# One merge of three edits: split first gathers, the last block written out with one linear half moved behind its squares, and a new order around the expert weights

## The chip, the cores and the metric

The kernel runs on one core of one Trainium2 chip. The metric is the device time of one execution in microseconds (us), the median of three runs. Engines are named as the profile names them: PE (TensorE, matrix products), DVE (VectorE), ACT (ScalarE), POOL (GpSimd) and SP (SyncE, which here only issues transfers).

## The reference

Input x has 64 samples of 64 x 512 numbers, which is 4096 rows of 512. Cut to what matters:

```
# layer 0
w   = weights[subjects]                         # 8 matrices of 64 x 64, one chosen for each sample
y   = einsum('bct,bcd->bdt', x, w)              # the "mix"
gu  = y @ ternary(w_gate_up).T                  # 512 -> 4096, gate and up
h   = silu(gate) * up                           # 2048 wide
x1  = x + rms_norm(h) @ ternary(w_proj).T       # 2048 -> 512
# layer 1
h   = x1 @ W.T + scal * (x1 @ A_b.T) @ B_b.T    # a linear layer, with one of 8 adapters per sample
logits = (h @ router_w.T + router_b)            # for each of 512 outputs, 8 experts
c   = per token: sum over the outputs of the renormalised top-2 weights, for each of 8 experts
out = x1 + sum_e c[t, e] * (h[t] @ expert_w[e].T + expert_b[e])
```

## The kernel before

Every float32 product is made of two or three products of rounded parts: a value is split into a high part and a remainder (`_hi`, `_lo`), so each large product is a chain of PE matmuls of 128 x 512, with a weight load each. ACT writes the high part (a copy), DVE subtracts it to get the low part. Nothing is scheduled by a tool. Each of the five engines has its own instruction list, written by hand in the order of the code, and semaphores counted in program order set who waits for whom. The numbers that the waits use for the two PSUM slots of stage 1 come from the lists `FIRST`, `SECOND`, `REST` and `TAIL` through `use(i, name)`: the n-th use of the slots may be written when use n-2 has been drained.

**Stage 1 (to about 900 us).** The 4096 rows go in 8 blocks of 512. For one block i, PE does `mix(i)` (L1420), then 16 hidden chunks `gu(i, j)` (L1445, 16 matmuls each), each followed by `proj(i, j-1)` (L1458, 8 matmuls), and in between the layer-1 linear part of block i-1: `turn` (transposes, L1477), `adapt` (L1487) and the two halves of `linear` (L1498 to L1504, 30 matmuls each), at j = 5 and j = 7. ACT and DVE store each half with `store_h` and `split_h`: ACT copies the high part, DVE subtracts, and ACT issues four transfers of 256 KB to `h_scratch`. After the last chunk come `proj(i, 15)`, `squares(i)` (L1467, the sum for the norm) and DVE's `finish(i)` (L1099, L1103), which takes an inverse root from POOL and writes x1. Blocks 0 and 1 are written out; in them the ternary weights are made (`quant`, L1430 on PE, with ACT and DVE). Blocks 2 to 7 are a loop on PE, DVE and ACT.

At the very start SP issues eight small gathers of the 64 x 64 matrices of block 0 (`gather_mix`, L415 to L417: a register load and a transfer for each sample), then two weight loads, the x rows of block 1, and eight gathers for block 1. ACT loads its first two function tables where it first needs them.

**Passage to stage 2 (898 to 942 us).** When the last `gu` has been drained SP loads 8 MB of router weights (`rraw`, one MB for each expert) over the old stage-1 weights. ACT and DVE split them (L830, L1198) while PE finishes block 7: transposes, the first group of router products, adapter, both linear halves.

**Stage 2 (to about 1628 us).** 32 tiles of 128 rows: PE makes router logits in PSUM planes (L1576 to L1580), ACT evacuates and seeds with the bias, DVE finds the top two of eight (`half`, L1267 to L1291), ACT and DVE pack them as bit codes (`stand`, `join`), and SP spills them.

**Passage to stage 3 and stage 3.** SP loads 8 MB of expert weights (`eraw`, L548). ACT and DVE split them (L913, L1332). Then 32 tiles again: PE makes eight expert products per tile (`experts`, L1618 to L1622, 12 matmuls per expert, 96 per tile), DVE adds each, scaled, to an accumulator (`expert`, L1371), ACT writes the expert bias back into the freed PSUM bank (`seed_expert`, L942), which is what PE waits for before it writes that bank again. In between DVE makes the scale factors of the tile after next (`decode`, L1236 to L1249, and eight times `total`, L1304). For tile 0 the bias isn't seeded: DVE adds it with eight instructions of its own (`bias`, L1353).

Of the kernel before, what the change touches and what calls it, by code (L numbers as in the profile page):

```python
# [29 lines left out]
P = 128  # L30
D = 512
# [73 lines left out]
TAIL = ["ss", "t0", "t1", "xa", "h0", "h1"]  # L105
# [24 lines left out]
def use(i, name):  # L130


    if isinstance(i, int):
        if i < 2 and f"{name}@{i}" in FIRST:
            n = FIRST.index(f"{name}@{i}")
        elif i == 0:
            n = FIRST.index(name)
        elif i == 1:
            n = len(FIRST) + SECOND.index(name)
        elif i == NBLK:  # L140
            n = len(FIRST) + len(SECOND) + (NBLK - 2) * len(REST) + TAIL.index(name)
        else:
            n = len(FIRST) + len(SECOND) + (i - 2) * len(REST) + REST.index(name)
# [18 lines left out]
def build(nc, x, idx7, idx6, cond_w, w_ffn, WcT, AT, Bt, scal, rwT, rb, ewT, eb, out):  # L162
# [7 lines left out]
    with root:  # L170
# [81 lines left out]

        bias_sb = sb("bias_sb", [P, 2, E, HO], F32, p2)
# [7 lines left out]
        c_ring = sb("c_ring", [P, 4, E], F32, p2)  # L261
        p3 = ExitStack()
        eb_sb = sb("eb_sb", [P, E, D], F32, p3)
# [4 lines left out]
        L = sb("L", [P, 2, E, HO], F32, p2)  # L268
# [35 lines left out]
        mixw_in = sem("mixw_in")  # L304
        xres_in = sem("xres_in")
# [21 lines left out]
        q_step = sem("q_step")  # L327
        mean_ready = sem("mean_ready")
# [63 lines left out]
        EWT = ewT.rearrange("(c p) (e o) -> e p c o", p=P, o=D)  # L392
# [19 lines left out]
        def _(sp):  # L412
            def gather_mix(i, w, done):
                for q in range(SPB):
# [25 lines left out]
            gather_mix(0, mixw, mixw_in)  # L440
# [116 lines left out]
            sp.wait_ge(decoded, 2)  # L557
            load_halves(2)
            spill(NT - 1, 1, 2 * NT - 1, 2 * NT, 2 * NT)

            def ahead(n, u, wait):

                if isinstance(n, int) and n == 0:
                    sp.wait_ge(bias_step, 1)
                else:
                    sp.wait_ge(exp_step, wait)
# [29 lines left out]
        def _(pool):  # L596
            nc.gpsimd.iota(adapter_i[:, :], pattern=[[0, 1]], base=0, channel_multiplier=1).then_inc(consts, 1)
# [20 lines left out]
        def _(act):  # L618
# [67 lines left out]
            def square(i, j, h):  # L686

                if not (first_block(i) and j == 0):
# [120 lines left out]
            with act.Fori(2, NBLK) as i:  # L809
                mix(i)  # L810
                for j in range(HC):
# [26 lines left out]
            split_router(1)  # L838
            store_x1(NBLK - 1)
# [10 lines left out]
            split_router(5)  # L850
            copy_h(NBLK - 1, 0)
# [79 lines left out]
            def store(n, u):  # L931
                act.wait_ge(exp_step, n * E + E)
# [12 lines left out]
            with act.Fori(0, NT // 2 - 1) as m:  # L945
                for u in range(2):
                    weigh(m * 2 + (u + 2), u, m + 1)
                    for e in range(E):
                        seed_expert(m * 2 + u, e)
                    store(m * 2 + u, u)  # L950
                    load_h(m * 2 + (u + 2), u)
            for e in range(E):
# [715 lines left out]
```

## Time and profile before

| | |
|---|---|
| median of three runs | 2350.64 us (2349.07 to 2351.0) |
| the profiled execution's own time | 2351.97 us |
| its span, first to last instruction | 2350.2 us |
| PE busy | 2301.7 us, 98% |
| DVE busy | 1669.3 us, 71% |
| ACT busy | 1148.8 us, 49% |
| mean granted TensorE clock | 0.995 |

The times of a row are microseconds from the start of the span. In a row of the timeline, the figure in brackets is how long the engine had stood idle before that row, and what released it. PE is idle for about 48 us in all, and nearly all of it lies in four places: the first 50 us, the end of block 7, the start of the experts, and the last 4 us.

### The profile page before, as it was taken

The page shows a single profiled execution, that of the slowest core. Times are in us where ns is not written, and L with a number is a line of the kernel's source. Part 1 is how long each engine was busy: PE and PEld are TensorE (multiplying, and loading weights), DVE is VectorE, ACT ScalarE, POOL GpSimd, SP SyncE. Part 2 cuts the span into 40 slices and gives each one's busy share as a digit, 9 for nine tenths or more (in the row PEclk, how much of TensorE's full clock was granted, in tenths as well). Part 3 has the DMA queues.
Part 4 walks back from the last instruction along what each step waited for, and adds up shares of the span by engine and source line. Part 5 has one row for each costly group of instructions (what it writes and reads, how often), then busy time and mean ns, then how long its engine had stood idle before and what let it go on. Part 6 is the DMA issues. An engine that isn't in the chain of part 4 may idle for free.

```text
span 2350.2 us, 30421 instructions
## 1 busy us (share of the span) xinstructions
PE 2301.7 (98%) x10280; PEld 1897.4 (81%) x10288; DVE 1669.3 (71%) x2497; ACT 1148.8 (49%) x1685; POOL 8.9 (0%) x16
## 2 busy tenths in 40 slices
PE   6999999999999999999999999998899999999999
PEld 5777888888888887888888888887688888888887
DVE  7985434334343435888888888999988888888883
ACT  6764333323332324788888888887322222222221
POOL 0000000000000000000000000000000000000000
PEclk9999999999999999999999999999999999999999
DMA  5314202111111115211111111215322222222220
GB/s 197 105 44 137 74 19 74 43 54 51 54 54 37 71 36 201 75 65 62 62 54 66 58 58 63 67 62 182 142 91 87 94 78 78 94 80 76 94 80 22
DMA packets 106589, 184.61 MB, mean 79 GB/s; under 512 B 12466, under 2 KB 45746, under 8 KB 105266
## 3 DMA queue, kind: packets, MB, share of 16 engines
q1 hardware_dynamic: 54946, 124.84, 15.2%
q10 hardware_dynamic: 51600, 59.25, 7.6%
q8 instruction: 20, 0.33, 0.1%
q14 instruction: 23, 0.19, 0.0%
HBM read 122.72 MB, written 61.34 MB: 78 GB/s over the span
## 4 chain that ended last, share of the span: by engine, by line
PE 90%; issue 5%; DVE 3%; ACT 1%; DMA 1%; ACTq 0%; SPq 0%; POOL 0%; POOLq 0%; DVEq 0%
PE slot L1445 17%; PE plane L1576 10%; PE plane L1578 10%; PE plane L1580 10%; PE ex L1618 10%; PE ex L1620 10%; PE ex L1622 10%; PE pj L1458 8%; PE slot L1498 3%; PE slot L1420 1%; PE slot L1487 1%; PE slot L1477 1%; PE slot L1430 0%; DMA eraw<-in_ewT 0%; DMA eb_sb<-in_eb 0%
## 5 line engine op out<-in xcount | busy, mean ns | idle before, releaser
L1618 PE MATMUL ex<-ew_hi,hb 128*128 128x512 f32 x1024 | 400.8, 391 | 16.6 <-DVE ew_lo L1332 11.3
L1445 PE MATMUL slot<-y_hi,wgu 128*128 128x512 f32 x1024 | 403.1, 394 | 2.3 <-DVE q_scale L1002 1.2
L1576 PE MATMUL plane<-rw_hi,hb 128*128 128x512 f32 x1024 | 399.5, 390 | 1.6 <-ACT plane L834 0.9
L1620 PE MATMUL ex<-ew_hi,hb 128*128 128x512 f32 x1024 | 400.4, 391 | 0.0
L1622 PE MATMUL ex<-ew_lo,hb 128*128 128x512 f32 x1024 | 400.3, 391 | 0.0
L1578 PE MATMUL plane<-rw_hi,hb 128*128 128x512 f32 x1024 | 399.2, 390 | 0.0
L1445 PE MATMUL slot<-y_lo,wgu 128*128 128x512 f32 x1024 | 399.1, 390 | 0.0
L1580 PE MATMUL plane<-rw_lo,hb 128*128 128x512 f32 x1024 | 399.1, 390 | 0.0
L942 ACT ACTIVATE ex<-eb_sb 128x512 f32<-128x512 f32 x248 | 149.3, 602 | 460.0 <-DVE acc L1371 395.8
L1304 DVE SCALAR_TENSOR_TENSOR lead_in<-code_in,wts 128x1024 bf16<-128x1024 bf16 x256 | 311.5, 1217 | 1.8 <-DVE code_in L1249 0.4
L1618 PEld LDWEIGHTS ex<-ew_hi,hb 128*128 128x128 f32 x1024 | 193.4, 189 | 58.5 <-issue 7.9
L1044 DVE TENSOR_TENSOR hid<-gate,slot 128x512 f32<-128x512 f32 x112 | 76.9, 687 | 222.8 <-ACT gate L673 222.1
L1445 PEld LDWEIGHTS slot<-y_hi,wgu 128*128 128x128 f32 x1024 | 192.3, 188 | 46.0 <-DVE q_scale L1002 4.3
L673 ACT ACTIVATE gate<-slot 128x512 f32<-128x512 f32 x128 | 76.5, 598 | 310.6 <-PE slot L1445 263.4
L1576 PEld LDWEIGHTS plane<-rw_hi,hb 128*128 128x128 f32 x1024 | 192.7, 188 | 42.4 <-ACT plane L834 1.3
L1622 PEld LDWEIGHTS ex<-ew_lo,hb 128*128 128x128 f32 x1024 | 193.5, 189 | 40.5
L1620 PEld LDWEIGHTS ex<-ew_hi,hb 128*128 128x128 f32 x1024 | 193.4, 189 | 40.2
L1580 PEld LDWEIGHTS plane<-rw_lo,hb 128*128 128x128 f32 x1024 | 192.7, 188 | 40.2
L1578 PEld LDWEIGHTS plane<-rw_hi,hb 128*128 128x128 f32 x1024 | 192.8, 188 | 40.0
L1445 PEld LDWEIGHTS slot<-y_lo,wgu 128*128 128x128 f32 x1024 | 192.3, 188 | 39.7
L862 ACT ACTIVATE L<-plane 128x512 f32<-128x512 f32 x256 | 150.5, 588 | 109.6 <-PE plane L1580 104.2
L1371 DVE SCALAR_TENSOR_TENSOR acc<-ex,c_ring,acc 128x512 f32<-128x512 f32 x193 | 144.5, 748 | 69.8 <-PE ex L1622 66.9
(128 smaller groups left out, 3148.3 us busy)
## 6 DMA issues: line engine op xcount, KB each, us to landing
hb<-h_scratch SPq DMA_DIRECT2D x34, 512.0 KB, 3.3
h_scratch<-ht ACTq DMA_DIRECT2D x64, 256.0 KB, 3.0
code_scratch<-half_code SPq DMA_DIRECT2D x64, 256.0 KB, 2.0
half_in<-code_scratch SPq DMA_DIRECT2D x32, 512.0 KB, 3.3
hb<-h_scratch ACTq DMA_DIRECT2D x30, 512.0 KB, 3.6
q_raw<-in_w_ffn SPq DMA_DIRECT2D x21, 512.0 KB, 3.4
x_scratch<-x_res ACTq DMA_DIRECT2D x8, 1024.0 KB, 4.4
rraw<-in_rwT SPq DMA_DIRECT2D x8, 1024.0 KB, 11.0
```

The lines of the kernel that those rows point to most:

```text
L862: nc.scalar.activation(L[:, s, 2 * b:2 * b + 2, :], plane[b][:, :, :], ACT.Copy).then_inc(evac, 1)
L942: nc.scalar.activation(ex[e][:, :], eb_sb[:, e, :], ACT.Copy).then_inc(ex_seeded, 1)
L1304: nc.vector.scalar_tensor_tensor(lead_in[:, k % 2, :].bitcast(BF16).rearrange("p (a n) -> p a n", a=2), code_in[:, k % 2, :, :], float(2 * ...
L1371: nc.vector.scalar_tensor_tensor((res if e == E - 1 else acc)[:, u, :], ex[e][:, :], c_ring[:, k, e:e + 1], base[:, u, :], ALU.mult, ALU.a ...
L1445: last = mm(slot[s % 2][:, g, :], wgu[:, c, r * P:(r + 1) * P], y[:, c, :], start=(c == 0 and v == 0), stop=(c == DC - 1 and v == 1))
L1458: last = mm(pj[k][:, :], h[:, k * P:(k + 1) * P], wpj[:, w, :], start=(j == 0 and v == 0), stop=(j == HC - 1 and v == 1))
L1576: mm(plane[b][:, :, :], hb[:, u, c, 0, :], rw_hi[:, w, c, o], start=False, stop=False, skip_group_check=True)
L1578: mm(plane[b][:, :, :], hb[:, u, c, 1, :], rw_hi[:, w, c, o], start=False, stop=False, skip_group_check=True)
L1580: last = mm(plane[b][:, :, :], hb[:, u, c, 0, :], rw_lo[:, w, c, o], start=False, stop=True, skip_group_check=True)
L1618: mm(ex[e][:, :], hb[:, u, c, 0, :], ew_hi[:, e, c, :], start=(first and c == 0), stop=False, skip_group_check=True)
L1620: mm(ex[e][:, :], hb[:, u, c, 1, :], ew_hi[:, e, c, :], start=False, stop=False, skip_group_check=True)
L1622: last = mm(ex[e][:, :], hb[:, u, c, 0, :], ew_lo[:, e, c, :], start=False, stop=(c == DC - 1), skip_group_check=True)
```

## The change

The layout of the lists is changed so that block 7 is numbered apart. Its loop trip is written out on PE, DVE and ACT (`block(NBLK - 1)`), without the second linear half of block 6, which each of the three engines now does after the squares of block 7. The first gathers are shared between SP and POOL, ACT's Silu table is loaded first, and SP's first transfers are reordered. The expert weights are laid out so that one expert's 1 MB is contiguous for each partition; they are loaded in one run. In the first expert tile PE does all products with the high part of the weights first, and then those with the low part. DVE adds the expert bias of tile 0 after its expert sums, and the packing of the last two router halves, the decoding and the totals of tile 2 follow. Buffers are moved so that the bias table of the experts lies over that of the router and can be loaded earlier.

```diff
-TAIL = ["ss", "t0", "t1", "xa", "h0", "h1"]
+LAST = [name for name in REST if name != "h1"]
+TAIL = ["ss", "last h1", "t0", "t1", "xa", "h0", "h1"]
...
-            gather_mix(0, mixw, mixw_in)
+            gather_mix(0, mixw, mixw_in, range(SPB // 2))
...
+            sp.dma_start(x_res[:, :, :], one(XB, 1)).then_inc(xmix1_in, 16)
+            gather_mix(1, mixw1, mixw1_in, range(3))
             load_raw(3)
             load_raw(4)
-            sp.dma_start(x_res[:, :, :], one(XB, 1)).then_inc(xmix1_in, 16)
-            gather_mix(1, mixw1, mixw1_in)
+            gather_mix(1, mixw1, mixw1_in, range(3, SPB))
...
-                    sp.dma_start(eraw[:, e, :, :], EWT[e]).then_inc(eraw_in[e], 16)
-                if b == 0:
-                    spill(NT - 2, 0, 2 * NT - 3, 2 * NT - 2, 2 * NT - 2)
+                    sp.dma_start(eraw[:, e, :, :].rearrange("p c o -> p (c o)"), ewT[e]).then_inc(eraw_in[e], 16)
             load_h(1, 1)
-            sp.wait_ge(joined, 2 * NT)
-            sp.dma_start(xin[:, 0, :], X1T[0]).then_inc(x1_in[0], 16)
+            sp.wait_ge(seeded, NT * PT)
             sp.dma_start(eb_sb[:, :, :], eb).then_inc(eb_in, 16)
-            sp.dma_start(xin[:, 1, :], X1T[1]).then_inc(x1_in[1], 16)
+            spill(NT - 2, 0, 2 * NT - 3, 2 * NT - 2, 2 * NT - 2)
             load_lead(2, 0)
             sp.wait_ge(decoded, 2)
             load_halves(2)
+            sp.wait_ge(lead_ready, 2 * NT)
+            sp.dma_start(xin[:, 0, :], X1T[0]).then_inc(x1_in[0], 16)
+            sp.dma_start(xin[:, 1, :], X1T[1]).then_inc(x1_in[1], 16)
             spill(NT - 1, 1, 2 * NT - 1, 2 * NT, 2 * NT)
...
         def _(pool):
+            pool.wait_ge(dconst, 1)
+            pool.wait_ge(subject_in, 16)
+            for q in range(SPB // 2, SPB):
+                v = pool.value_load(subject_i[0:1, q:q + 1], min_val=0, max_val=E - 1)
+                r = (q % 2) * C
+                pool.dma_start(mixw[r:r + C, q // 2, r:r + C], cond_w[bass.ds(v * C, C), :]).then_inc(mixw0_in, 16)
...
+            act.wait_ge(dconst, 3)
+            nc.scalar.activation(sq[:, 0:1], ones_col[:, :], ACT.Silu).then_inc(table_in, 1)
             quant_in(0)
...
-            with act.Fori(2, NBLK) as i:
+            def block(i):
...
-                    if j == 7:
+                    if j == 7 and not isinstance(i, int):
                         store_h(i - 1, 1)
+
+            with act.Fori(2, NBLK - 1) as i:
+                block(i)
                 act.wait_ge(h_stored, i * 128)
+            block(NBLK - 1)
...
             split_router(0)
             split_router(1)
+            store_h(NBLK - 2, 1)
             store_x1(NBLK - 1)
...
             split_router(5)
+            act.wait_ge(h_stored, 128 * (NBLK - 1))
             copy_h(NBLK - 1, 0)
...
-            split_expert(2)
+            for e in range(2, E):
+                split_expert(e)
             stand(NT - 1, 0)
-            split_expert(3)
-            split_expert(4)
             stand(NT - 1, 1)
-            for e in range(5, E):
-                split_expert(e)
...
             finish(NBLK - 1)
             split_router(0)
+            split_h(NBLK - 2, 1)
             split_router(1)
...
+            for e in range(E):
+                expert(0, e, 0, 0)
+            for s in range(2):
+                join(NT - 1, s)
             dve.wait_ge(eb_in, 16)
+            dve.wait_ge(exp_step, E)
             for e in range(E):
-                bias(0, e, 0, 1)
-            for n in range(4):
+                bias(e)
+            decode(2, 2)
+            for e in range(E):
+                total(2, e, 2)
+            for n in range(1, 4):
                 tile(n, n, n // 2)
...
+            linear(NBLK - 2, 1)
             turn(NBLK - 1, 0)
...
+            def first_experts():
+
+                pe.wait_ge(hb_in[0], NT // 2 * 16 + 16)
+                for e in range(E):
+                    if e >= 4:
+                        pe.wait_ge(evac, NT * PT - 3 + e - 4)
+                    pe.wait_ge(ehi, e + 1)
+                    for c in range(DC):
+                        for v in range(2):
+                            mm(ex[e][:, :], hb[:, 0, c, v, :], ew_hi[:, e, c, :], start=(c == 0 and v == 0), stop=False)
+                for e in range(E):
+                    pe.wait_ge(elo, e + 1)
+                    for c in range(DC):
+                        last = mm(ex[e][:, :], hb[:, 0, c, 0, :], ew_lo[:, e, c, :], start=False, stop=(c == DC - 1))
+                    last.then_inc(ex_filled, 1)
```

The order of ACT at the end of block 7, before: the router weights' high parts, the store of x1 (`x_scratch`), the first seed (`plane`), the two turns.

```order
L830 ACTIVATE rw_hi<-rraw 128x2048 x2
L749 DMA x_scratch<-x_res 128x4x512
L834 ACTIVATE plane<-bias_sb 128x512
L717 ACTIVATE x1t_hi<-slot 128x1024 x2
L830 ACTIVATE rw_hi<-rraw 128x2048 x2
```

The same place now:

```order
L849 ACTIVATE rw_hi<-rraw 128x2048 x2
L744 ACTIVATE ht<-slot 128x2x512
L753 DMA h_scratch<-ht 128x4x128 x4
L762 DMA x_scratch<-x_res 128x4x512
L853 ACTIVATE plane<-bias_sb 128x512
L730 ACTIVATE x1t_hi<-slot 128x1024 x2
L849 ACTIVATE rw_hi<-rraw 128x2048 x2
```

The copy of the moved half and its four transfers stand ahead of the store of x1, the seed and the turns.

The order of DVE from the low parts of the expert weights (`ew_lo`) to the second tile, before (the first part of `half`, nine rows, left out; L1353 is the bias, L1371 an expert sum, L1304 a total):

```order
L1230 TENSOR_TENSOR half_code<-sgn 128x1024
L1286 TENSOR_TENSOR L<-L,m 128x1024
L1287 TENSOR_TENSOR L<-L,m 128x1024
L1291 TENSOR_TENSOR lead<-m 128x256
L1332 TENSOR_TENSOR ew_lo<-eraw,ew_hi 128x2048 x2
L1230 TENSOR_TENSOR half_code<-sgn 128x1024
L1332 TENSOR_TENSOR ew_lo<-eraw,ew_hi 128x2048 x3
L1353 SCALAR_TENSOR_TENSOR acc<-eb_sb,c_ring,xin 128x512
L1353 SCALAR_TENSOR_TENSOR acc<-eb_sb,c_ring,acc 128x512 x7
L1371 SCALAR_TENSOR_TENSOR acc<-ex,c_ring,acc 128x512
L1236 TENSOR_TENSOR half_in<-half_in 128x2x512
```

The same place now:

```order
L1325 TENSOR_TENSOR lead<-m 128x256
L1366 TENSOR_TENSOR ew_lo<-eraw,ew_hi 128x2048 x5
L1395 SCALAR_TENSOR_TENSOR acc<-ex,c_ring,xin 128x512
L1395 SCALAR_TENSOR_TENSOR acc<-ex,c_ring,acc 128x512 x7
L1264 TENSOR_TENSOR half_code<-sgn 128x1024 x2
L1380 SCALAR_TENSOR_TENSOR acc<-eb_sb,c_ring,acc 128x512 x7
L1380 SCALAR_TENSOR_TENSOR res<-eb_sb,c_ring,acc 128x512
L1270 TENSOR_TENSOR half_in<-half_in 128x2x512
```

The expert sums of tile 0 stand ahead of the two joins (`half_code`) and of the bias, and the totals that stood between them follow in one run.

## Rows read from the trace of the kernel before

**Rows 1.** Waits of PE: total us, times, longest us.
```profile
PE ex L1618 <- DVE ew_lo L1332: 11.3, 2, 7.3
...
PE ex L1618 <- ACT ex L942: 5.3, 2, 3.2
```
**Rows 2.** Stretches: us; busy PE, PEld, DVE, ACT, POOL; clock; DMA share; GB/s.
```profile
50.00:100.00 50.00, 49.73 (x217) 39.04 (x220) 45.47 (x68) 36.53 (x48) 0.00 (x0) 1.00 0.33 111
...
912.00:914.00 2.00, 2.00 (x6) 1.56 (x5) 2.00 (x3) 2.00 (x2) 0.00 (x0) 0.50 1.03 430
```
**Rows 3.** Timeline of the start: SP, PE, DVE, ACT.
```profile
3.02 9.36 SPq L417 DMA_DIRECT2D mixw<-in_cond_w  x8
...
10.22 1.04 PE L1430 MATMUL slot<-q_mag,group_mean 128*128 128x512 bf16 x2 [3.95 <-DMA mixw<-in_cond_w]
13.98 5.70 PE L1420 MATMUL slot<-mixw,x_mix 128*128 128x128 f32 x32 [2.72 <-issue]
...
15.46 0.69 DVE L1030 TENSOR_TENSOR q_res<-q_res,q_sign 128x1024 bf16<-128x1024 bf16 x1
28.36 0.69 DVE L1044 TENSOR_TENSOR hid<-gate,slot 128x512 f32<-128x512 f32 x1 [0.97 <-ACT gate L673]
...
26.44 1.28 ACT L673 ACT_TABLE_LOAD   x1
```
**Rows 4.** Tile mixw in the first 45 us: its gathers' time to landing.
```profile
DMA to landing us min/median/max: 1.8/2.6/6.4
```
**Rows 5.** Timeline, end of block 7: PE, then ACT.
```profile
906.62 3.68 PE L1477 MATMUL slot<-ident,x_res 128*128 128x128 f32 x16 [4.10 <-DVE x_res L1103]
...
916.03 0.40 PE L1487 MATMUL slot<-x1t_hi,a_hi 128*128 128x512 f32 x1
...
942.03 0.50 PE L1576 MATMUL plane<-rw_hi,hb 128*128 128x512 f32 x1 [0.88 <-ACT plane L834]
...
926.02 1.03 ACT L731 ACTIVATE ht<-slot 128x1024 fp32r<-128x1024 f32 x1 [0.47 <-PE slot L1504]
930.71 3.72 ACT L830 ACTIVATE rw_hi<-rraw 128x2048 fp32r<-128x2048 f32 x2 [3.66 <-issue]
```
**Rows 6.** Chain of waits: twelve matmuls of a linear half.
```profile
278.79 2.80 PE slot L1498 x12
```
**Rows 7.** Tile x_scratch: time to landing of its transfers.
```profile
DMA to landing us min/median/max: 2.5/2.9/16.5
```
**Rows 8.** Timeline of DVE, from the expert weights to tile 1.
```profile
1628.17 1.22 DVE L1304 SCALAR_TENSOR_TENSOR lead_in<-code_in,wts 128x1024 bf16<-128x1024 bf16 x1
...
1629.32 4.49 DVE L1332 TENSOR_TENSOR ew_lo<-eraw,ew_hi 128x2048 fp32r<-128x2048 f32 x2
...
1637.37 1.22 DVE L1267 TENSOR_TENSOR top<-L 128x1024 f32<-128x1024 f32 x1
...
1646.73 4.48 DVE L1332 TENSOR_TENSOR ew_lo<-eraw,ew_hi 128x2048 fp32r<-128x2048 f32 x2
1651.13 0.68 DVE L1230 TENSOR_TENSOR half_code<-sgn 128x1024 uint16<-128x1024 uint16 x1
1652.84 6.69 DVE L1332 TENSOR_TENSOR ew_lo<-eraw,ew_hi 128x2048 fp32r<-128x2048 f32 x3 [1.03 <-ACT ew_hi L913]
...
1660.89 5.48 DVE L1353 SCALAR_TENSOR_TENSOR acc<-eb_sb,c_ring,acc 128x512 f32<-128x512 f32 x7
...
1671.64 0.75 DVE L1371 SCALAR_TENSOR_TENSOR acc<-ex,c_ring,acc 128x512 f32<-128x512 f32 x1
...
1684.27 0.75 DVE L1371 SCALAR_TENSOR_TENSOR acc<-ex,c_ring,xin 128x512 f32<-128x512 f32 x1
...
1689.49 0.75 DVE L1371 SCALAR_TENSOR_TENSOR acc<-ex,c_ring,acc 128x512 f32<-128x512 f32 x1
```
**Rows 9.** Timeline of PE in the first expert tiles.
```profile
1673.07 0.52 PE L1618 MATMUL ex<-ew_hi,hb 128*128 128x512 f32 x1 [2.14 <-ACT ex L942]
...
1696.58 0.39 PE L1618 MATMUL ex<-ew_hi,hb 128*128 128x512 f32 x1
```

More of the change, by code:

```diff
@@ L139, in use @@
             n = len(FIRST) + SECOND.index(name)
-        elif i == NBLK:
-            n = len(FIRST) + len(SECOND) + (NBLK - 2) * len(REST) + TAIL.index(name)
+        elif i == NBLK or (i == NBLK - 1 and name == "h1"):
+            n = len(FIRST) + len(SECOND) + (NBLK - 3) * len(REST) + len(LAST) + TAIL.index(name if i == NBLK else "last h1")
+        elif i == NBLK - 1:
+            n = len(FIRST) + len(SECOND) + (NBLK - 3) * len(REST) + LAST.index(name)
         else:
@@ L412, in _, with gather_mix @@
         def _(sp):
-            def gather_mix(i, w, done):
-                for q in range(SPB):
+            def gather_mix(i, w, done, samples=range(SPB)):
+                for q in samples:
                     v = sp.value_load(subject_i[0:1, bass.ds(i * SPB + q, 1)], min_val=0, max_val=E - 1)
@@ L686, in square @@
             def square(i, j, h):
-                if not (first_block(i) and j == 0):
+                if first_block(i) and j == 0:
+                    act.wait_ge(table_in, 1)
+                else:
                     act.wait_ge(ss_ready, i * HC + j)
@@ L1180, in _, with block @@
                     split_h(0, 1)
-            with dve.Fori(2, NBLK) as i:
+            def block(i):
                 mix(i)
@@ L1191, in _ @@
                         split_h(i - 1, 0)
-                    if j == 7:
+                    if j == 7 and not isinstance(i, int):
                         split_h(i - 1, 1)
+            with dve.Fori(2, NBLK - 1) as i:
+                block(i)
+            block(NBLK - 1)
             def split_router(e):
@@ L1336, in _, with bias @@
                 split_expert(e)
-            half(NT - 1, 1, 1, NT // 2 - 1)
-            split_expert(3)
-            split_expert(4)
-            join(NT - 1, 1)
-            for e in range(5, E):
-                split_expert(e)
-            def bias(n, e, k, trip):
-                u = k % 2
-                if e == 0:
-                    dve.wait_ge(x1_in[u], trip * 16)
-                    dve.wait_ge(summed, n * E + E)
-                else:
-                    dve.wait_ge(bias_step, n * E + e)
-                nc.vector.scalar_tensor_tensor(acc[:, u, :], eb_sb[:, e, :], c_ring[:, k, e:e + 1],
-                                               (xin if e == 0 else acc)[:, u, :], ALU.mult, ALU.add).then_inc(bias_step, 1)
+            half(NT - 1, 1, 1, NT // 2 - 1, joins=False)
+            for e in range(3, E):
+                split_expert(e)
+            def bias(e):
+                if e:
+                    dve.wait_ge(bias_step, e)
+                nc.vector.scalar_tensor_tensor((res if e == E - 1 else acc)[:, 0, :], eb_sb[:, e, :], c_ring[:, 0, e:e + 1],
+                                               acc[:, 0, :], ALU.mult, ALU.add).then_inc(bias_step, 1)
             def expert(n, e, k, trip):
                 u = k % 2
-                base = acc
+                first = isinstance(n, int) and n == 0
                 if e != 0:
                     dve.wait_ge(exp_step, n * E + e)
-                elif isinstance(n, int) and n == 0:
-                    dve.wait_ge(bias_step, E)
                 else:
@@ L1370, in expert @@
                     dve.wait_ge(out_done[u], trip * 16)
-                nc.vector.scalar_tensor_tensor((res if e == E - 1 else acc)[:, u, :], ex[e][:, :], c_ring[:, k, e:e + 1],
-                                               base[:, u, :], ALU.mult, ALU.add).then_inc(exp_step, 1)
+                nc.vector.scalar_tensor_tensor((res if e == E - 1 and not first else acc)[:, u, :], ex[e][:, :],
+                                               c_ring[:, k, e:e + 1], (xin if e == 0 else acc)[:, u, :],
+                                               ALU.mult, ALU.add).then_inc(exp_step, 1)
             def tile(n, k, pair):
@@ L1546, in _, with block @@
                     linear(0, 1)
-            with pe.Fori(2, NBLK) as i:
+            def block(i):
                 mix(i)
@@ L1560, in _ @@
                         linear(i - 1, 0)
-                    if j == 7:
+                    if j == 7 and not isinstance(i, int):
                         linear(i - 1, 1)
+            with pe.Fori(2, NBLK - 1) as i:
+                block(i)
+            block(NBLK - 1)
             proj(NBLK - 1, HC - 1)
```

50 lines of the change are left out of this document (26 added, 24 removed).

## The prediction

> **What bounds the kernel now.** I read four views, in this order. The page's busy times name PE as the engine that is nearly always at work, so a change can only win what PE stands idle, or what it loses at a low clock. The waits of PE say what it stands idle for: in [rows 1] the reader is to see two waits for the low parts of the expert weights, 11.3 us together, and two for a PSUM bank that ACT has to seed again, 5.3 us. The view by stretches says where there is nothing to win: PE is busy for 49.73 of the 50 us from 50 to 100 [rows 2], and all over the loops. The timelines of the start, of the end of block 7 and of the first expert tiles then say what ends each wait last. I call a time "old" when it is read on the clock of the trace before.
>
> **Start: gain 2.5 us.** SP issues the eight gathers of block 0 in 9.36 us, 1.17 each, and PE starts the mix at 13.98, after 2.72 us of idleness [rows 3]. Now SP and POOL issue four each. SP's last is issued at 3.02 + 3 x 1.17 = 6.5. POOL issues no transfer anywhere in the trace, so its pace is bounded. At SP's pace and the median landing of 2.6 us [rows 4] all are in at 9.1; but PE itself is busy with the second mean until 11.26 [rows 3], so the mix can start at 11.3 at best, a gain of 2.7. At worst its transfers come only after DVE's run of bf16 instructions, which ends at 15.46 + 0.69 = 16.15 [rows 3]: 16.15 + 2.6 = 18.8, a loss of 4.8. I take a landing near the longest one, 6.0 of the 6.4 us [rows 4], since the weight loads, the x rows and all eight gathers now fall into the same ten microseconds: 6.5 + 6.0 = 12.5, a gain of 1.5. It is nearer to the good end because the only rows of such a gather are SP's. Everything behind follows the mix: ACT and DVE split its output, then go on without a wait for a load.
>
> The tables: ACT loads one at 26.44, 1.28 us, ahead of the first gate, and DVE is idle for 0.97 us before the product with it [rows 3]. Now the table with Silu is loaded first, where the other one was loaded before, and the load at 26.44 is gone. DVE has its own work up to the start of that idleness, so 1.0 us is won and not 1.28. The new one-column Silu delays ACT's first copy by some tenths, which the later wait for the second weight load covers. From there DVE and PE work in step until 50 us, and after it PE is 49.73 of 50 us busy [rows 2], so both gains are passed on: 1.5 + 1.0 = 2.5. If the cover of the first tenths is gone, it costs these tenths.
>
> [...]
>
> **End of block 7: gain 3.1 us.** A linear half is 30 matmuls: 12 take 2.80 us [rows 6], so it is 7.0 us. It goes out of block 7, so all up to the last squares comes 7.0 us earlier, and goes in after the squares, at old 902.5, just where PE waits 4.10 us for x1 [rows 5]. It ends at old 909.5. The first transposes follow (x1 is ready at 906.6), but the second ones need the slot of the moved half drained, and ACT now has to do this half's copy, wait for DVE, and issue four transfers ahead of the seed and the turns. Such a copy started at 926.02 and ACT's next compute instruction at 930.71, so this costs ACT 4.69 us [rows 5]: 909.5 to 914.2, then x1's transfer, about 0.4, the seed, 0.6, and PE's first router group starts at old 915.3. PE has stood idle for some 4 of the 5 us up to there, as much as before 906.62, where the granted clock went to the lower level: at 912 to 914 it is 0.50, and only 6 matmuls start in 2 us [rows 2], where 2.80/12 us each would give 8.6. So I let the group of 12 take 4.3 us. The adapter starts at 919.6; before, it started at 916.03 [rows 5], where the same low clock had slowed the group. Delay 3.6 us. It is carried on: ACT's copy of the next half at 926.02 + 3.7, its loads' high parts 4.69 later, the same chain up to the seed that PE waits for at 942.03 [rows 5], which comes 3.7 to 3.9 us later. Net gain 7.0 - 3.9 = 3.1. If the clock stays high, ACT's chain begins at its two turns and the delay is 2.6: gain 4.4, the upper bound. The lower bound: ACT's next copy now waits for the moved half's transfers to land (they share the buffer). They are issued at old 911.8 to 914.1 into 8 MB of router weights under way; a transfer of x1 issued there needed 16.5 us where 2.9 is the median [rows 7]. 914.1 + 16.5 = 930.6 against 929.7 when it is wanted: a cost of up to 1 us, or 3 us if 1 MB more makes it longer. Lower bound 0.
>
> The Trainium skill, "DMA: Bandwidth & Descriptors", section "Queues, rings and completion order", says that a DMA engine takes turns between the queues packet by packet. The 16.5 us agree with it: x1's packets are smaller than those of the router weights. The packets of the moved half are smaller still (512 bytes of 128 numbers); by this rule it lands last of all, which is rival 2.
>
> **The experts: gain 6.8 us.** Before, PE takes an expert only when its low part is there, and DVE does `half` (1637.37 to 1646.73, 9.36 us) between the third and the fourth low part [rows 8]. Now PE does the 64 high products first, for which ACT's copies suffice, and the low ones as DVE delivers. What then ends last is DVE, and it is busy without a gap, so I add it up from old 1629.32 [rows 8]: three low parts 6.7; `half` without its join 9.36 - 0.6 = 8.8; five low parts 11.1 (up to here 1655.9); eight expert sums at the pace of dependent ones, 5.48/7 = 0.78, 6.3; two joins 1.3; eight of the bias 6.3; decoding 3.4 (the 5.22 below less a sum and a total); eight totals at 1.25, 10.0; this gives 1683.2 for the first expert sum of tile 1, which stood at 1684.27. The second one comes 5.22 later as before (1684.27 to 1689.49), at 1688.4. The seed lies between DVE and PE: DVE's sum at 1671.64, PE at 1673.07, 1.4 us [rows 8, 9]. So PE can start the second expert of tile 2 at 1689.8. Before, it started it at 1696.58 [rows 9], being late itself: it had lost 11.3 + 5.3 us [rows 1] and more at the low clock. The gain is 6.8. PE isn't what ends last: low products done at about 1657, plus 96 matmuls at 0.23, is 1679; it then waits some 5 us for the first seed of tile 2 (1683.2 + 1.4 = 1684.6). Its clock will fall after that, and 12 matmuls at 0.43 us, double 0.21, take 5.1 and end at 1689.7, just when the second seed comes. From there DVE takes 5.22 us once and about 1.8 for each further expert of a tile, which is less than PE's 12 x 0.23 = 2.8, and no wait is left. The weights: 8 MB contiguous, the last 2 MB no later than before; DVE needs the last one at 1653.7. The x1 rows are now asked for at old 1644.7 and needed at 1655.9, behind about 4 MB; if they are late it costs up to 2 us. Bounds 4 and 7.5 us.
>
> **Sum.** 2.5 + 3.1 + 6.8 = 12.4 us. The profiled execution took 2351.97 us, 1.3 more than the median of 2350.64; it would take 2339.6. The median of three becomes 2338.2.
>
> **Rivals.** 1: POOL's descriptors wait for DVE. The mix starts at 18.8, the start costs 4.8 - 1.0 = 3.8 instead of winning 2.5; total gain 3.1 + 6.8 - 3.8 = 6.1, 2344.5 us. For it: DVE's bf16 instructions up to 16.15 [rows 3]; against: each gap between two of them is a chance to get in. 12%. 2: the moved half holds up ACT, by its landing or its place, and block 7 gives nothing: gain 9.3, 2341.3 us. For it the 16.5 us; against, 929.7 is almost late enough. 13%. 3: the run of bias and totals ahead of tile 1 holds PE longer than I sum, because x1's rows or the decoding's inputs land late behind 4 MB, and the low clock then stretches over the second expert: the experts give 3, total 8.6, 2342.0 us. 10%. 4, the other side: block 7 as straight code has to be fetched by three engines, and they starve for instructions. It would have to cost more than 12.4 us to undo the gains, and 17.1 to be measured as slower, in a block of about 100 us (some 426 large matmuls at 0.23). Against it: the stretch from 50 to 100 us is straight code too, and PE is busy for 49.73 [rows 2]. 4%, at some 2360 us. 5: the change does little, since what it wins is lost to waits not seen: 3%, 2349 us. My forecast, all three gains within their middle: 58%.
>
> **How the numbers follow.** About 0.2%, 4.7 us, is what a measurement of this kernel can tell from no change. Forecast and rivals 1 to 3 are all faster by more than that, but for their tails: 88%. Within 0.2%: rival 5 and the tail of rival 1 in company of 2, 7%. Slower: rival 4 and what I don't see, 5%. The range: rivals 1 and 3 inside, best case 2.7 + 1.0 + 4.4 + 7.5 = 15.6 us, 2335.0. From 2334.3 to 2346.0 about one in ten is left out above and less than that below.
>
> **What would show it.** Start: the mix on PE at 11.3 to 13 and one table load on ACT before the gates; at 18 or later rival 1 is right. Block 7: no wait for x1 before the transposes, a wait of about 2.5 us before the first router group, the wait before the second half's groups about 1 us. Experts: 64 high products with waits under 1 us, low ones at DVE's pace of 2.2 us, then one wait of 5 us before tile 2, and DVE without a gap. I am wrong if PE waits in tile 2 for more than the first two experts, or if block 7 isn't shorter by 7 us up to its last squares.

## The result and the profile after

The changed kernel takes 2346.94 us, median of 22 runs (2345.03 to 2350.4); the kernel before takes 2350.61 us beside it (22 runs, 2349.07 to 2352.16). The ratio is 0.9986, 95% interval 0.9979 to 0.9992: 3.3 us less (1.9 to 4.9; the two medians are 3.7 apart), which is within the 0.2% that I had called "no change". The forecast was 2338.2 us with a range up to 2346.0, so three quarters of the expected gain are missing. The profiled execution after took 2350.2 us (span 2348.5), near the slow end of its spread; before it was 2351.97 (span 2350.2), so between the two traces only 1.7 us are gained.

Two places divide the trace into three: A, where PE starts the adapter of block 0 (201.71 before), and B, where it starts the router's second half (s=1, 942.03 in [rows 5]). After, timeline of PE:

```profile
11.90 6.09 PE L1455 MATMUL slot<-mixw,x_mix 128*128 128x128 f32 x32 [0.51 <-DMA mixw<-in_cond_w]
...
200.04 0.47 PE L1522 MATMUL slot<-x1t_hi,a_hi 128*128 128x512 f32 x1 [1.80 <-DVE x1t_lo L1138]
...
902.45 1.03 PE L1512 MATMUL slot<-ident,x_res 128*128 128x128 f32 x8
905.08 1.06 PE L1512 MATMUL slot<-ident,x_res 128*128 128x128 f32 x8 [1.59 <-DVE ht L1157]
915.52 0.76 PE L1615 MATMUL plane<-rw_hi,hb 128*128 128x512 f32 x1 [9.38 <-ACT plane L853]
...
947.32 0.50 PE L1615 MATMUL plane<-rw_hi,hb 128*128 128x512 f32 x1 [1.19 <-ACT plane L853]
```

Up to A it is 1.67 us shorter, from B to the end 6.99 us shorter (1401.18 against 1408.17), and from A to B 6.96 us longer, where I had forecast 3.1 us less. The sum is the 1.7 us. The waits of PE say the same: the two for low parts of [rows 1], 11.3 us, are 1.9 now, the ones for `ex` are about as long as before, five short ones for ACT's high parts of these weights are new (3.4 us, the longest 1.8), and so is a long one for the seed of the first router group.

```profile
PE plane L1615 <- ACT plane L853: 10.6, 2, 9.4
PE ex L1653 <- ACT ex L962: 5.8, 3, 4.8
...
PE ex L1672 <- DVE ew_lo L1366: 1.9, 2, 1.0
```

What holds the seed up is in ACT's timeline (ACTq is the issuing of transfers on ACT):

```profile
902.65 1.02 ACT L744 ACTIVATE ht<-slot 128x1024 fp32r<-128x1024 f32 x1 [2.28 <-PE slot L1539]
904.96 8.67 ACTq L753 DMA_DIRECT2D h_scratch<-ht  x4
913.67 1.06 ACTq L762 DMA_DIRECT2D x_scratch<-x_res  x1
914.78 0.60 ACT L853 ACTIVATE plane<-bias_sb 128x512 f32<-128x512 f32 x1 [11.11 <-issue]
...
931.33 1.03 ACT L744 ACTIVATE ht<-slot 128x1024 fp32r<-128x1024 f32 x1 [0.82 <-PE slot L1539]
933.65 2.31 ACTq L753 DMA_DIRECT2D h_scratch<-ht  x4
```

The four transfers of the moved half take 8.67 us to issue; the same four of the next half take 2.31. By itself each shows that it is the fourth: the first three take 0.38, 0.53 and 0.53 us, the last, in the group below, 7.14.

```profile
L753 ACTq DMA_DIRECT2D h_scratch<-ht x12: 378/532/7141, 905.0 to 945.2; - x12
```

Meanwhile the loads of the router weights fill the DMA engines. The queues between 905 and 910 us, SP's is q1 and ACT's q10 (packets, MB, share), and two stretches as in [rows 2]:

```profile
q1 hardware_dynamic: 286, 2.08, 99.5%
q10 hardware_dynamic: 77, 0.04, 2.6%
```
```profile
908.00:912.00 4.00, 0.00 (x0) 0.00 (x0) 0.00 (x0) 0.00 (x0) 0.00 (x0) 0.50 1.02 421
916.00:920.00 4.00, 4.00 (x11) 3.03 (x10) 3.29 (x3) 4.00 (x4) 0.00 (x0) 0.50 1.10 368
```

ACT's queue moves 0.04 MB in five microseconds, though it has up to 1 MB to move. PE, DVE and ACT all stand still from 908 to 912, and after it PE works at the lower level of its clock (0.50) to about 921: the twelve matmuls of the group start 0.43 us apart and take 5.26 us, to the adapter's first at 920.78.

### The profile page after: what moved, and what is told of

Its sections match the earlier page's. It is cut to its first block, busy times and chain, and to the rows that moved or that the text cites. A ratio compares the mean times of both kernels' runs of the same rounds, so it can differ in the third digit from the quotient of the medians.

```text
span 2348.5 us, 30271 instructions
## 1 busy us (share of the span) xinstructions
PE 2302.6 (98%) x10280; PEld 1895.4 (81%) x10288; DVE 1670.0 (71%) x2497; ACT 1148.0 (49%) x1685; POOL 11.2 (0%) x20
## 4 chain that ended last, share of the span: by engine, by line
PE 94%; DVE 3%; DMA 1%; ACT 1%; issue 1%; ACTq 1%; SPq 0%; DVEq 0%
PE slot L1480 20%; PE plane L1615 10%; PE plane L1617 10%; PE plane L1619 10%; PE pj L1493 9%; PE ex L1653 9%; PE ex L1655 9%; PE ex L1654 9%; PE slot L1533 4%; PE slot L1455 1%; PE slot L1522 1%; DMA eraw<-in_ewT 1%; ACTq L753 1%; PE slot L1512 0%; DVE lead_in L1338 0%
## 5 line engine op out<-in xcount | busy, mean ns | idle before, releaser
L1653 PE MATMUL ex<-ew_hi,hb 128*128 128x512 f32 x992 | 386.9, 390 | 5.8 <-ACT ex L962 5.8
L1654 PE MATMUL ex<-ew_hi,hb 128*128 128x512 f32 x992 | 386.4, 390 | 0.0
L1655 PE MATMUL ex<-ew_lo,hb 128*128 128x512 f32 x992 | 386.4, 390 | 0.0
L1653 PEld LDWEIGHTS ex<-ew_hi,hb 128*128 128x128 f32 x992 | 186.6, 188 | 45.8 <-ACT ex L962 6.4
L1654 PEld LDWEIGHTS ex<-ew_hi,hb 128*128 128x128 f32 x992 | 186.6, 188 | 38.7
L1655 PEld LDWEIGHTS ex<-ew_lo,hb 128*128 128x128 f32 x992 | 186.5, 188 | 38.8
```

The lines of the kernel that those rows point to most:

```text
L1653: mm(ex[e][:, :], hb[:, u, c, 0, :], ew_hi[:, e, c, :], start=False, stop=False, skip_group_check=True)
L1654: mm(ex[e][:, :], hb[:, u, c, 1, :], ew_hi[:, e, c, :], start=False, stop=False, skip_group_check=True)
L1655: last = mm(ex[e][:, :], hb[:, u, c, 0, :], ew_lo[:, e, c, :], start=False, stop=(c == DC - 1), skip_group_check=True)
```

## The experiments

Each part alone and taken out, then the moved half's transfers in other places. Medians in us; A, B and "A to B" are read from the profiled execution of each. A ratio is to the kernel before, measured beside it: its medians were 2351.23 us for e1 to e4, 2350.99 for e5, e6, e9 and e10, and 2351.78 for e7, e8, e11 and e12.

| kernel | median | ratio to before, 95% | A | B | A to B |
|---|---|---|---|---|---|
| before | 2350.61 | | 201.71 | 942.03 | 740.32 |
| changed | 2346.94 | 0.9986 (0.9979 to 0.9992) | 200.04 | 947.32 | 747.28 |
| e1, block 7 undone | 2341.40 | 0.9960 (0.9946 to 0.9974) | 200.19 | 938.35 | 738.16 |
| e2, block 7 alone | 2356.49 | 1.0023 (1.0014 to 1.0032) | 202.85 | 947.75 | 744.90 |
| e3, sends later on ACT | 2339.07 | 0.9951 (0.9938 to 0.9965) | 198.17 | 935.68 | 737.51 |
| e4, sends on SP | 2339.03 | 0.9953 (0.9939 to 0.9966) | 198.20 | 935.36 | 737.16 |
| e5, three there | 2338.38 | 0.9947 (0.9932 to 0.9962) | 198.53 | 934.61 | 736.08 |
| e6, loads held | 2346.16 | 0.9978 (0.9968 to 0.9987) | 200.40 | 944.32 | 743.92 |
| e7, start alone | 2347.72 | 0.9983 (0.9974 to 0.9992) | 199.92 | 938.10 | 738.18 |
| e8, experts alone | 2343.76 | 0.9966 (0.9952 to 0.9979) | 201.78 | 942.08 | 740.30 |
| e9, eight halves | 2346.88 | 0.9984 (0.9975 to 0.9993) | 197.92 | 942.78 | 744.86 |
| e10, group between | 2338.89 | 0.9953 (0.9939 to 0.9966) | 198.50 | 936.00 | 737.50 |
| e11, sends ahead | 2335.24 | 0.9931 (0.9917 to 0.9944) | 199.77 | 933.51 | 733.74 |
| e12, between, on ACT | 2338.37 | 0.9945 (0.9931 to 0.9958) | 197.98 | 934.67 | 736.69 |

### The parts apart: e1, e2, e7, e8

e1 is the changed kernel with block 7 as before, e2 the kernel before with this part alone (the same edit the other way round), on all engines:

```
-                    if j == 7 and not isinstance(i, int):
+                    if j == 7:
                         linear(i - 1, 1)
...
-            linear(NBLK - 2, 1)
             turn(NBLK - 1, 0)
```

This is PE's share; `store_h` on ACT and `split_h` on DVE go the same way.

> The changed kernel with its second part undone: the half linear(6, 1) is back in block 7. Theory A (the fourth transfer of the moved half is held up at its issue on ACT for 7.1 us, since 8 MB of router weights are under way; PE stands idle for 9.4 us; the move costs about 5.3 us): start and experts keep their gains, 2350.6 - 1.7 - 7.1 = 2341.8 us, some 5 us less than the changed kernel; PE waits 4.1 us for x1 before the first transposes as before. Theory B (the long issue is an accident of the one profiled execution, and the rest of the gain went to stretches at the low clock): the move gives its 3.1 us in the median, so without it 2350 us. Theory C (the end of block 7 is worth nothing either way): 2347.

> The kernel before with the move of linear(6, 1) alone, nothing of the start and of the experts. Theory A: the fourth issue takes about 7 us again, PE waits some 9 us for the first seed, and the time is 2350.6 + 5.3 = 2355.9 us. Theory B: 2350.6 - 3.1 = 2347.5 us. Theory C: 2350.6.

Measured: 2341.40 and 2356.49 us, 0.4 less and 0.6 more than theory A gives. Without the move the kernel is faster by 5.5 us than with it; the move alone makes the kernel before slower by 5.3 us (3.3 to 7.5). In the trace of e2 the four issues take 8.68 us and PE waits again:

```profile
906.10 8.68 ACTq L743 DMA_DIRECT2D h_scratch<-ht  x4
```
```profile
916.49 0.77 PE L1594 MATMUL plane<-rw_hi,hb 128*128 128x512 f32 x1 [9.21 <-ACT plane L841]
```

So the long issue is no accident of one execution: theories B and C fall. e7 is the kernel before with `gather_mix(0, ..., range(SPB // 2))`, POOL's four gathers and the early Silu alone; e8 has only the edits at the experts.

> The kernel before with the part at the start alone (four gathers of block 0 on POOL, the Silu table first, the order of SP's first loads). Forecast of the prediction: 2.5 us less, 2348.3. In the traces of the kernels with this part PE reaches the first product of the second block's adapter 1.3 to 1.7 us sooner than before (201.7 us) where a stretch after the mix ran at the low clock, and 3.2 to 3.8 us sooner where it didn't: 2347 to 2349.5. Rival: what the start wins is given back later, 2351.

> The kernel before with the part at the experts alone. Forecast of the prediction: 6.8 us less, 2344.1; the trace of the changed kernel gives 7.1, 2343.8. Rival (the low clock or late rows of x1 eat it): 2347.5 or more.

Measured: 4.0 us less (1.9 to 6.1) for the start, 8.0 us less (4.9 to 11.3) for the experts. Neither is given back later. But the trace of e7 has only 1.8 us of its gain at A; 2.1 more come at the end of block 7, where nothing was changed. There PE waits the same 4.10 us for x1, but is back at the full clock when the first router group starts:

```profile
904.82 3.29 PE L1493 MATMUL slot<-ident,x_res 128*128 128x128 f32 x16 [4.10 <-DVE x_res L1117]
909.26 0.47 PE L1592 MATMUL plane<-rw_hi,hb 128*128 128x512 f32 x1 [1.15 <-issue]
...
912.11 0.40 PE L1503 MATMUL slot<-x1t_hi,a_hi 128*128 128x512 f32 x1
```

The twelve matmuls take 2.85 us, where they take 4.96 in the kernel before (911.07 to 916.03). e1 has the same (2.82 us), e8 has not (4.97). No run shows why the clock came back sooner, so these 2.1 us can't be credited to the edit at the start. They are not in the changed kernel either, whose group takes 5.26 us behind its wait of 9.38. With the 5.3 us of e2 the three parts give 6.7 us less, against 3.3 (1.9 to 4.9) for the whole; without the 2.1 it would be 4.6, inside the interval.

### Why the fourth issue waits: e5, e6, e9

e5 leaves three of the transfers where they are and moves the fourth:

```
-            store_h(NBLK - 2, 1)
-            store_x1(NBLK - 1)
+            copy_h(NBLK - 2, 1)
+            send_h(NBLK - 2, 1, (0, 1, 2))
...
             split_router(3)
+            send_h(NBLK - 2, 1, (3,))
+            store_x1(NBLK - 1)
             adapt(NBLK - 1)
```

> The changed kernel, but ACT issues only three of the four transfers of the moved half ahead of the seed and the turns; the fourth and x1's follow behind the third and fourth high parts of the router weights. Theory A (ACT's queue takes three such transfers, and holds the engine at the next one until they have drained): the three take 0.4 + 0.5 + 0.5 us, PE waits some 2.5 instead of 9.4 us before the first group, and the time is 2338 to 2341 us. Theory A2 (each issue is slow in the loaded queues, the order doesn't matter): ACT is still held up for 6 us or more ahead of the seed, PE waits over 7 us, 2346 us.

```profile
901.76 1.53 ACTq L755 DMA_DIRECT2D h_scratch<-ht  x3
903.34 0.60 ACT L855 ACTIVATE plane<-bias_sb 128x512 f32<-128x512 f32 x1 [2.87 <-issue]
903.48 7.02 ACTq L755 DMA_DIRECT2D h_scratch<-ht  x1
903.87 1.92 ACT L730 ACTIVATE x1t_hi<-slot 128x1024 fp32r<-128x1024 f32 x2
905.68 3.72 ACT L851 ACTIVATE rw_hi<-rraw 128x2048 fp32r<-128x2048 f32 x2
```

The three take 1.53 us, and the fourth is held for 7.02 again; but it stands behind the seed, the turns and two copies in the program, and these run during it. PE waits 1.15 us for the seed. 2338.38 us, 8.6 less than the changed kernel, by the place of one transfer. e6 leaves the order and takes away the loads in flight:

```
                 if e == 1:
                     sp.wait_ge(proj_done, NBLK * HC)
                     load_h(0, 0)
+                    sp.wait_ge(h_stored, 128 * (NBLK - 1))
```

> The changed kernel, but SP starts the router weights of experts 2 to 7 only when the four transfers of the moved half have landed. If the loads in flight are what drains ACT's queue slowly (theory A): the four issues take about 2.3 us, PE waits about 2.5 us before the first group, and the loads now come later, the last at about 910 + 15 = 925 us, which costs some us behind the adapter: 2338 to 2342 us. If the number of transfers alone holds the fourth (theory A3): the fourth issue takes 7 us again, and the time is over 2350 us.

```profile
903.63 2.31 ACTq L754 DMA_DIRECT2D h_scratch<-ht  x4
...
915.92 1.92 ACT L850 ACTIVATE rw_hi<-rraw 128x2048 fp32r<-128x2048 f32 x1 [6.57 <-DMA rraw<-in_rwT]
```
```profile
q10 hardware_dynamic: 1962, 0.98, 67.3%
```

The mechanism is right: with nothing else in flight the four go out in 2.31 us, and between 903 and 908 us ACT's queue moves 0.98 MB in 1962 packets. The time is a miss, 2346.16 where I had expected 2342 at most: the loads start at 908.84, ACT stands 6.57 us for the third weight, and PE 4.4 us for the adapter's low part. e9 cuts each of the four in two:

```
+                            for g in range(2):
+                                act.dma_start(HB[l, 2 * u + b, v][:, 2 * g:2 * g + 2, :],
+                                              ...).then_inc(h_stored, 16)
```

> The changed kernel with each of the four transfers of the moved half cut into two of half the size (8 transfers, 256 packets of 512 bytes each instead of 512). If what fills up is a number of packets or descriptors: six go at once (0.4 to 0.5 us each) and the seventh is held for about 7 us, total about 10 us, 2348 us. If it is a number of transfers: the fourth is held already, and the rest also, but the queue's work is the same: total 9 to 12 us, with the long issue at the fourth.

Five halves go out in 0.38 to 0.51 us each, the sixth takes 4.37, the seventh 1.68, the eighth 0.65; all eight 9.29 us, and the time is unchanged, 2346.88. Neither branch of the expectation is met: it is the sixth that is held, not the fourth and not the seventh. So what the queue takes at once is not a number of transfers; three whole ones (1536 packets of 512 bytes), but five halves (1280), don't fit a fixed number of packets either, and what the limit counts stays open.

### The transfers elsewhere: e3, e4

In both only `copy_h(NBLK - 2, 1)` is left in the place of `store_h`. e3 puts the transfers behind ACT's copies of the router weights:

```
             split_router(3)
+            send_h(NBLK - 2, 1)
             adapt(NBLK - 1)
```

e4 gives them to SP, behind its loads:

```
             load_h(1, 1)
+            sp.wait_ge(drained, l1_use(NBLK - 2, "h1")[0] + 1)
+            for b in range(2):
+                for v in range(2):
+                    sp.dma_start(HB[NBLK - 2, 2 + b, v], ...).then_inc(h_stored, 16)
```

> The changed kernel, but ACT issues the four transfers of the moved half later: behind the first seed, both turns and the third and fourth high parts of the router weights; its copy stays. Theory A: the first group starts at about 907.5 us instead of 915.5, the adapter at about 910, and PE gets to the groups of the second half (s=1) at about 936 instead of 947.3: 2346.9 - 11.5 = 2335.4 us, if the four issues take 2.3 us there. If the fourth is held up in the new place as well (x1's transfer and three others ahead of it in ACT's queue), the copies behind it come up to 7 us later: 2341 us. Theory B: at most 2 us less than the changed kernel, 2345. Theory C: 2347.

> The changed kernel, but SP issues the four transfers of the moved half, behind its own router weights; ACT only copies. Theory A: ACT is held up by nothing; the first group at about 907.5 us, the adapter at 910, 2335.4 us, unless the landing behind the 8 MB on SP's queue is later than about 920 us, where ACT's next copy waits for it. Theory B: 2345. Theory C: 2347.

Both take 2339 us: 7.9 less than the changed kernel, not the 11.5 expected. In e3 x1's transfer goes first, and now the third of the moved half is held, for 8.14 us: again the fourth on the queue (x1's, 1 MB, was issued 3.5 us ahead of the other three), under ACT's compute. In e4 it is SP that is held (four issues in 11.36 us), which nobody waits for. The missing 3.6 us are PE's clock, as e10 will show. PE's first group starts at 903.70 in e4; 907.5 was expected on the clock of the changed kernel's trace, where the first transposes stand 3.5 us later (902.45 against 898.92), so this is as forecast. But it runs at half the clock, and the adapter's product is masked at 912.32 instead of some 909:

```profile
904.00:908.00 4.00, 4.00 (x10) 3.13 (x10) 4.00 (x3) 3.27 (x2) 0.00 (x0) 0.50 1.01 414
```

Matmuls start 0.43 us apart there, at the full clock 0.23. PE had worked 2.1 of the 4.8 us before, on two rows of small transposes with waits of 1.59 and 1.09 us.

### Without the low clock: e10, e11, e12

e10 is e4 with the group between the turns (PE), the second router weight's low part ahead of the split (DVE), and the third one's between the turns (ACT, DVE):

```
             turn(NBLK - 1, 0)
+            group(0, 0, 0, 0, 0, first=True)
             turn(NBLK - 1, 1)
-            group(0, 0, 0, 0, 0, first=True)
```

> The changed kernel with SP issuing the moved half's transfers, and the order at the end of block 7 changed: on PE the first router group stands between the two turns, and the adapter waits for the second turn's low part only at its seventh product; on DVE the low part of router weight 1 stands ahead of the split of the moved half, and that of weight 2 between the turns; on ACT the high part of weight 2 between the turns. Theory: what is left of the loss there is PE's 2.7 us of idleness and the half clock that follows (24 matmuls in 8.5 instead of 5.6 us). Without it the adapter ends at about 908.3 instead of 912.3 us, gain up to 4.1: 2335.0 us, unless ACT's copy then waits for the landing of the moved half at about 918 us: gain 1.2, 2337.8. Rival: the clock falls all the same, 2338.

The clock stays at 1.00 from 904 to 908, and DVE masks the adapter's product at 909.15 instead of 912.32. But ACT's next copy then waits for the landing of the moved half, which shares its buffer:

```profile
920.01 1.03 ACT L749 ACTIVATE ht<-slot 128x1024 fp32r<-128x1024 f32 x1 [4.33 <-DMA h_scratch<-ht]
```

PE pays for it further on, with a wait of 2.61 us (at 931.17) for the low part of a router weight, whose high part ACT writes behind that copy and its transfers. That was the "unless": 2338.89 us, where I had 2337.8. e11 lets SP issue the four ahead of the last two router weights (`if e == 5:` in the loop over the weights), e12 lets ACT issue them, three behind the first turn.

> The kernel with the group between the turns, but SP issues the moved half's four transfers ahead of the router weights of experts 6 and 7, and of the rows of tile 1 of h. There ACT's copy waited 4.3 us for the landing of these transfers, at 920.0. Theory: 2 MB fewer ahead of them, they land some 4 us sooner, the copy comes at about 915.7, 2338.9 - 4.3 = 2334.6 us. Rival: the four still share the engines with the weights, whose packets are 8 KB against 512 bytes, and land no sooner, or the weights of expert 7 come too late: 2338 to 2340.

> The same group between the turns, but ACT issues the transfers: three behind its first turn, the fourth and x1's behind the high part of router weight 3. On ACT's queue such transfers landed 13.6 us after issue, issued at 902.7, so at about 916.5: the copy waits until then, 2338.9 - 3.5 = 2335.4 us. Rival: the fourth issue (7 us) holds ACT at the adapter's high part, up to 909.5 or later, and it lands at 920 as well: 2339 to 2341.

```profile
917.40 1.03 ACT L750 ACTIVATE ht<-slot 128x1024 fp32r<-128x1024 f32 x1 [0.53 <-PE slot L1548]
```

In e11 they land 8.8 to 10.3 us after issue instead of up to 15.1, the copy waits for PE alone, and the kernel takes 2335.24 us: 16.5 less than before in the same comparison (13.2 to 19.5), and the best of all. In e12 the three issues behind the first turn (1.53 us) hold the third weight's copy up to 902.96 (901.88 in e10). Behind it on DVE stands the second turn's low part, for which PE now waits 2.54 us (0.98 in e10), and the clock falls again (0.63 from 908 to 912); this costs what the landing gives: 2338.37. The fourth issue is held too, for 5.48 us, but the second turn runs meanwhile. Its expectation failed by 3 us: the rival had the time nearly right, but the harm came through the turn and not through the adapter's high part.

## Why the prediction was wrong, step by step

- **Start, 2.5 us.** The mechanism is right, and 2.5 lies in the interval measured for this part alone, 4.0 us (1.9 to 6.1); but in its trace 2.1 us of that came from the clock at the end of block 7, and 1.8 from the start itself. The mix starts at 11.90 (forecast 12.5, from 13.98), POOL issues its four gathers 1.15 us apart, the first at 3.90, and the product of the first gate comes at 26.67 (28.36 in [rows 3]). Rival 1 is false: POOL's gathers land 4.3 to 5.7 us after issue, SP's four 4.6 to 6.4. DVE's first bf16 instruction with two inputs starts only at 7.72, inside the last of POOL's issues; I had looked at where DVE's run ends (16.15) and not at where it begins.

```profile
3.90 0.70 POOL L606 DMA_DIRECT2D mixw<-in_cond_w  x1 [3.33 <-issue]
5.08 0.52 POOL L606 DMA_DIRECT2D mixw<-in_cond_w  x1 [0.49 <-issue]
6.22 0.52 POOL L606 DMA_DIRECT2D mixw<-in_cond_w  x1 [0.61 <-issue]
7.36 0.52 POOL L606 DMA_DIRECT2D mixw<-in_cond_w  x1 [0.62 <-issue]
```

  The Trainium skill ("SBUF — State Buffer", "Who interferes with whom") says that a VectorE instruction with two SBUF inputs contends with a GpSimd instruction that reads SBUF, not with one that only writes it, and that `tensor_tensor`, which all these bf16 instructions with two inputs are, has no two-port mode. By that they would not hold up the writing of descriptors. Only the last gather overlaps one of them here, and it landed within the 5.7 us of all four; that agrees, as far as one overlap can. What I hadn't priced is the clock: in five of the eleven traces with this part a stretch behind the mix runs low, and A is reached at 199.77 to 200.40; in the other six at 197.92 to 198.53. From 15 to 30 us, changed kernel and e9:

```profile
15.00:30.00 15.00, 11.17 (x47) 8.31 (x47) 11.57 (x15) 11.42 (x13) 0.00 (x0) 0.89 0.56 189
```
```profile
15.00:30.00 15.00, 10.81 (x56) 8.08 (x55) 13.51 (x18) 13.30 (x15) 0.00 (x0) 1.00 0.54 182
```

- **End of block 7, 3.1 us: the step that failed.** "ACT now has to do this half's copy, wait for DVE, and issue four transfers", 4.69 us from a row in which no load was in flight [rows 5], and 0.4 for x1's transfer behind it. Here the two take from 902.65 to 914.78, 12.1 us: 7.0 more, of which the fourth issue alone is 6.4 (7.14 against 0.75 of the same fourth before) and x1's 0.7 (1.06 against 0.39). I had seen that these transfers fall "into 8 MB of router weights under way", and drew from it only that they would land late (rival 2, which had the place right and the price wrong: it took the 3.1 us away, and in fact they turned into a loss of 5.3, 8.4 us in all). A landing is waited for by one copy 20 us later; an issue stands in the stream of the engine, ahead of the seed. The next 1.0 us is the group, for which I had let 4.3 us: it took 5.26. I had taken the 6 matmuls of the stretch in [rows 2] for six starts, but the view counts the one under way as well; starts were 0.43 us apart there too, and twelve are 5.1. Besides, in the profiled execution a second stretch ran low behind A, from 200.8 to 204.1 us; the twelve matmuls from A on took 4.42 us there, 2.88 before, and this 1.5 us belongs to no part of the change. Up to the last squares the block is shorter as forecast (894.56 against 901.57: 7.0 us, of which 1.7 came from the start and 1.5 were lost to that stretch). And the moved half's landing, the other side of rival 2, cost nothing: 12.2 to 12.8 us after issue, and ACT's next copy at 931.33 waited for PE. Rival 4 (fetching of straight code) isn't seen: PE's only wait ahead of the last squares is 0.98 us for DVE, the same as before, and e4, with the same straight block, takes 3.2 us less from A to B than the kernel before.
- **Experts, 6.8 us.** Right: 6.99 us in the trace, 8.0 (4.9 to 11.3) alone. The chain of DVE came out by its terms, from the three low parts to the first sum of tile 1 it took 53.5 us for 53.9 summed, without a gap of note; PE waits 4.80 us at the first seed of tile 2, as forecast 5, and 0.80 at the second. Rival 3 is false. One sign failed without harm: the 64 high products were to wait under 1 us each, and the last expert's waited 1.77, since its weights landed late (ACT waited 1.92 us for them); DVE ended last all the same.

```profile
1634.61 6.69 DVE L1366 TENSOR_TENSOR ew_lo<-eraw,ew_hi 128x2048 fp32r<-128x2048 f32 x3
...
1650.10 11.09 DVE L1366 TENSOR_TENSOR ew_lo<-eraw,ew_hi 128x2048 fp32r<-128x2048 f32 x5
1661.10 0.74 DVE L1395 SCALAR_TENSOR_TENSOR acc<-ex,c_ring,xin 128x512 f32<-128x512 f32 x1
...
1688.10 0.75 DVE L1395 SCALAR_TENSOR_TENSOR acc<-ex,c_ring,xin 128x512 f32<-128x512 f32 x1
```
```profile
1689.53 0.79 PE L1653 MATMUL ex<-ew_hi,hb 128*128 128x512 f32 x1 [4.80 <-ACT ex L962]
...
1694.76 0.50 PE L1653 MATMUL ex<-ew_hi,hb 128*128 128x512 f32 x1 [0.80 <-ACT ex L962]
```

- **The range.** Its worst case for block 7 was "nothing gained", for the landing. A bound below zero was missing, though the row it rested on stood in quiet queues and the moved transfers would not. With 5.3 us lost instead of 3.1 won, the same sum gives 2350.6 + 5.3 - 2.5 - 6.8 = 2346.6, near the time measured. That it comes so near is partly luck: with the 4.0 and 8.0 us of the parts alone it would be 2343.9.

What stays open: how much such a queue holds (e9 fits neither transfers nor packets), what sets off the low stretch behind the mix in some executions and not in others, and why the group of block 7 found the full clock in e1 and e7 behind the same wait.

## What to carry to other kernels

A transfer has two prices, the landing and the issue, and the issue is paid by the engine that issues it. Where a queue shares the DMA engines with large loads, price the issue from a row with such loads in flight, or put the transfers behind all that others wait for, or on an engine that has nothing else to do. And a gain of place (7 us of work into a gap of 4) is only as good as the shortest thing moved along with it: look at what the moved step issues, not only at what it computes.

## What the hardware showed

- With 1 MB loads in flight on SP's queue (7.3 KB a packet, 2.08 MB in 286), ACT's queue took three transfers of 512 packets in 1.4 to 1.5 us and held the engine at the fourth: 7.14 us in the changed kernel, 7.11 in e2, 7.02 in e5, 5.48 in e12, against 0.75 us with quiet queues. In e3, with x1's 1 MB first, it was 8.14. SP's own queue does the same (e4, longest 9.48 us).
- In that time ACT's queue got 77 of 363 packets. The Trainium skill ("DMA: Bandwidth & Descriptors", "Queues, rings and completion order") has the engines take turns between queues packet by packet, a packet being typically 9 to 17 descriptors. Whether the packets that the profile counts are these, no run here shows, so the row can't confirm turn for turn. What it shows is 2% of the bytes moved for the queue with the small packets.
- Compute instructions that stand ahead of a held issue in the program still run while it is held (e5: the turns and two copies start inside the 7.02 us), those behind it don't.
- Two waits of PE, 1.59 and 1.09 us, around two rows of small transposes were followed by the lower clock level over the next 5 us (e4: 0.50); with a group of 12 matmuls between the transposes it stayed at 1.00 (e10, e11), but fell to 0.63 in e12, behind a wait of 2.54 us.
